# Attention with geometric and dot heads: V blocks two half-steps back everywhere, turns behind them, rows of maxima on GpSimd's queue

## The chip, the cores and the metric

The kernel runs on one core of one Trainium2 chip. The metric is the device time of one execution in microseconds (us), lower is better; times are given as the median of the runs shown.

## The reference

One layer on x of 2 x 2048 x 256, all f32. Attention has 16 heads of 16 channels, causal, and each head attends twice over the same tokens:

```python
std_logits = einsum('bhqd,bhkd->bhqk', q, k) * scale
geo_logits = einsum('bqhi,bkhi->bhqk', read_lines, J_write) * inc_scale
std_out = softmax(mask(std_logits)) @ v
geo_out = softmax(mask(geo_logits)) @ geo_v
combined = (1 - gate) * std_out + gate * geo_out
x = layernorm(x + combined @ out_w + out_b)
x = layernorm(x + (silu(x @ wg.T) * (x @ wu.T)) @ wd.T)
```

`read_lines` and `J_write` are six numbers per head and token, made by products of four-vectors and scaled to length one.

## The kernel before

Three parts follow one another: `project` makes the operands and writes them to DRAM, `attend` computes both attentions, `finish` does the output product, the norms and the gated layer. The change is all in `attend`.

`attend` runs over 16 items (`ITEMS`): a batch and a pair of heads. An item has four query tiles of 512 columns; a query tile goes through its key blocks of 128 in steps, and a step has one or two groups. A group is called a half-step here and counted h = 0 to 35 (`PVS`, `NPV`). Most half-steps hold one key block and 512 query columns. The last three of a query tile lie on the diagonal: 512 columns, 384, and one that holds two blocks, of 256 and 128. The tiles end at h = 2, 9, 20 and 35 (`LAST_OF`), and each last step has one group only.

In a half-step TensorE (PE, `step`) computes the GEO scores (line 1036) and, for an item that comes later, one or two tiles of dot-product maxima (line 1074), then the DOT scores (line 1042). Scores of both heads stand in one of two PSUM buffers `ex`. ScalarE (ACT, line 1217) makes the exponentials of each, two per half-step, into one of eight buffers `prob`. On the diagonal GpSimd zeroes what the mask forbids (line 1004). PE then multiplies by V into PSUM `pv` (`times_v`, line 1131: the V block). Ahead of a tile's first V block it waits until VectorE (DVE) has taken the tile before out of `pv` (`take`, line 1303). Score matmuls wait until the exponential of the buffer is done, exponentials until V has read their buffer:

```python
def earlier(j):
    prev, ps = (at, s - 1) if s else (before, NSTEP - 1)
    if prev is not None and j < len(STEPS[ps][1]):
        times_v(*prev, ps, j, head)
```

So the V block of group j of the step before follows the scores of group j. Where a step has one group, both V blocks of the step before stand behind its scores, then comes that of its own in the next step's first half-step, and the second half-step of that step has none.

The softmax needs a bound on each query's DOT score. Maxima of key blocks are made on PE and reduced by DVE (lines 1233, 1236) for the item after. At half-steps 30 (EARLY, query tiles 0 to 2) and 9 (LATE, tile 3) there is a turn: DVE makes columns of negated maxima (`negm`), PE transposes them (line 1108), DVE casts the result to `mrow` (line 1295). The rows of `mrow` are then sent by four DMAs into rows of the query operands `gq` and `dq` (line 894), where the score matmul adds them. PE waits for EARLY's rows (`m_in[EARLY]`) ahead of the GEO scores of half-step 0 and for LATE's at half-step 21. In a turn there is a branch that is not taken with these inputs; it would compute maxima of GEO scores too.

The tiles of maxima and the turns use three PSUM banks in a ring (`Ring`), and each new use waits for the last one of its bank: the bank of the EARLY turn comes again a few tiles later, that of the LATE turn is that of the very next tile.

SyncE (SP) issues DMAs in a fixed order (`item` in `block.sync`): per item the stores of the four taken tiles, 24 operand loads and V for the item after the next, and the rows. The LATE rows stand after the store of tile 0, the EARLY rows at the end of an item, behind the last six operand loads:

```python
store(it, 2)
load(range(18, 24))
...
if it + 1 < ITEMS:
    rows(it + 1, EARLY, sets[(it + 1) % NSET])
```

GpSimd makes 24 masks an item and after tile 2's masks, in items 0 to 3, work put aside: in item 0 it loads the output weights, waits for them and loads a weight; in items 1 to 3 it converts a weight and loads the next.

## Time and profile before

| | us |
|---|---|
| median of 3 runs | 1793.87 |
| lowest, highest | 1790.86, 1795.01 |
| the profiled execution, its own time | 1791.5 |
| its span, first to last instruction | 1789.8 |
| busy: PE | 1609.8 |
| busy: ACT | 1217.1 |
| busy: DVE | 1073.1 |
| busy: GpSimd (POOL) | 337.2 |

The profile is of one execution. PE is busy for 90% of it, which is a mean over parts of different kinds: `attend`'s items run from about 278 to 1474 us, `project` before, `finish` after. A busy PE is not a PE at its peak, since the ends of pipelined matmuls are modelled; starts are measured. In a row of the timeline the word in brackets is the idle time ahead of the first instruction and what ended it; "issue" means that the profile shows nothing that was waited for.

### The profile page before, as it was taken

What the parts mean: (1) busy time and instruction counts of PE and PEld (TensorE: products, weight loads), DVE (VectorE), ACT (ScalarE), POOL (GpSimd) and SP (SyncE); (2) the same over time, 40 slices, a digit from 0 to 9 for tenths busy, and PEclk for the clock granted to TensorE, in tenths of its full rate; (3) what the DMA queues carried; (4) which work ended last, traced back from release to release, by engine and by line L of the source; (5) the groups of instructions that cost most, each with busy time, mean ns of one, the idle gap of its engine ahead of it and who ended that gap; (6) DMA issues with size and microseconds to landing.
All of it is one profiled execution on the core that took longest, in us unless ns stands there. A gap on an engine that the chain in (4) does not pass through costs nothing. (4 is left out here: it accounts for less than half of the span.)

```text
span 1789.8 us, 31799 instructions
## 1 busy us (share of the span) xinstructions
PE 1609.8 (90%) x11809; PEld 567.9 (32%) x11809; DVE 1073.1 (60%) x2621; ACT 1217.1 (68%) x1457; POOL 337.2 (19%) x479
## 2 busy tenths in 40 slices
PE   7897467998989999999999999999999988999997
PEld 4554212222222222222222222222222225555564
DVE  4775575665666666666667666666666514554433
ACT  3554406988979889888898888988889872112111
POOL 4432321211111111111101111111110133121000
PEclk9999658999999999999999999999999998999999
DMA  5665521221212112121121211212214013222000
GB/s 169 213 207 171 180 88 43 87 80 50 86 44 70 51 62 72 46 66 65 50 82 50 67 58 56 71 46 65 72 40 129 21 54 115 96 84 70 23 12 24
DMA packets 95579, 140.31 MB, mean 78 GB/s; under 512 B 6352, under 2 KB 64528, under 8 KB 93360
## 3 DMA queue, kind: packets, MB, share of 16 engines
q1 hardware_dynamic: 94208, 135.08, 22.9%
q0 software_dynamic: 624, 2.75, 0.6%
q8 instruction: 97, 1.59, 0.4%
q14 instruction: 74, 0.61, 0.1%
q10 hardware_dynamic: 576, 0.28, 0.1%
HBM read 81.96 MB, written 55.61 MB: 77 GB/s over the span
## 5 line engine op out<-in xcount | busy, mean ns | idle before, releaser
L1217 ACT ACTIVATE prob<-ex 128x1024 f32<-128x1024 f32 (+1 forms) x1152 | 1048.5, 978 | 193.2 <-PE ex L1036 183.2
L1236 DVE TENSOR_REDUCE mp<-mx 128x1 f32<-128x512 f32 x768 | 492.2, 685 | 257.9 <-PE mx L1074 257.7
L1131 PE MATMUL pv<-prob,va 128*32 128x512 f32 (+3 forms) x5120 | 576.5, 541 | 0.4 <-POOL prob L1004 0.4
L1004 POOL TENSOR_SCALAR_AFFINE_SELECT prob<-prob 128x256 f32<-128x256 f32 (+1 forms) x384 | 186.1, 485 | 1025.3 <-ACT prob L1217 1020.5
L1042 PE MATMUL ex<-dq,dk 34*128 34x512 bf16 (+7 forms) x2560 | 336.8, 349 | 24.6 <-ACT prob L1217 17.6
L1233 DVE CUSTOM_DVE_ANT_0 dull<-mx,mask_qk 128x128 f32<-128x128 f32 (+3 forms) x512 | 222.0, 487 | 127.2 <-PE mx L1074 127.1
L1036 PE MATMUL ex<-gq,gk 38*128 38x512 bf16 (+3 forms) x1280 | 219.5, 356 | 45.2 <-issue 18.8
L1074 PE MATMUL mx<-dk,dq 64*128 64x512 bf16 (+3 forms) x1280 | 228.0, 357 | 15.8 <-issue 12.4
L1036 PEld LDWEIGHTS ex<-gq,gk 38*128 38x128 bf16 x1280 | 56.8, 93 | 452.2 <-ACT prob L1217 372.8
L1131 PEld LDWEIGHTS pv<-prob,va 128*32 128x32 f32 x5120 | 114.3, 108 | 240.2 <-issue 217.5
L1561 ACT ACTIVATE sg<-pg 128x512 f32<-128x512 f32 x48 | 28.7, 597 | 219.7 <-PE pg L1501 219.5
L1042 PEld LDWEIGHTS ex<-dq,dk 64*128 64x128 bf16 (+1 forms) x2560 | 93.1, 94 | 190.5 <-ACT prob L1217 160.7
L574 POOL TENSOR_TENSOR sp<-d,sp 128x512 bf16<-128x512 f32 (+1 forms) x48 | 69.2, 1456 | 139.3 <-ACT sp L669 139.3
L1501 PE MATMUL pg<-y_t,wg_f 128*128 128x512 f32 x192 | 90.3, 593 | 1.1 <-ACT y_t L1544 1.1
L1517 PE MATMUL po<-wd_f,ht 128*128 128x256 f32 x384 | 85.0, 381 | 6.4 <-DVE ht L1629 6.4
L1501 PE MATMUL pg<-y_t,wu_f 128*128 128x512 f32 x192 | 90.2, 592 | 0.0
L593 PE MATMUL pn<-wv,xc 128*128 128x512 f32 x128 | 64.4, 628 | 23.5 <-DVE vn L745 15.7
L1074 PEld LDWEIGHTS mx<-dk,dq 64*128 64x128 bf16 x1280 | 65.7, 96 | 49.0 <-DVE mp L1236 14.4
L1629 DVE SCALAR_TENSOR_TENSOR ht<-pg,sg 128x512 f32<-128x512 f32 x48 | 33.0, 690 | 79.0 <-ACT sg L1561 79.0
L1517 PEld LDWEIGHTS po<-wd_f,ht 128*128 128x128 f32 x384 | 72.3, 190 | 18.3 <-issue 5.1
L612 PE MATMUL pr<-xc,wqk 128*128 128x512 f32 x128 | 62.1, 641 | 14.9 <-ACT sp L663 14.9
L1303 DVE COPY on<-pv 128x512 f32<-128x512 f32 x64 | 44.2, 691 | 34.6 <-PE pv L1131 34.6
(109 smaller groups left out, 906.1 us busy)
## 6 DMA issues: line engine op xcount, KB each, us to landing
values<-vn SPq DMA_DIRECT2D x32, 512.0 KB, 5.2
va<-values SPq DMA_DIRECT2D x16, 1024.0 KB, 18.5
raw<-on SPq DMA_DIRECT2D x64, 256.0 KB
parts_dot<-sp SPq DMA_DIRECT2D x32, 384.0 KB, 5.0
dq<-parts_dot SPq DMA_DIRECT2D x96, 128.0 KB
dk<-parts_dot SPq DMA_DIRECT2D x96, 128.0 KB
parts_geo<-sp SPq DMA_DIRECT2D x16, 288.0 KB, 2.8
gq<-parts_geo SPq DMA_DIRECT2D x96, 48.0 KB
```

Of the source, the lines that this page charges most:

```text
L574: g.tensor_tensor(out=sp3[m][0:n, SLOTS[m][2], :], in0=d32[m][0:n, :], in1=sp3[m][0:n, SLOTS[m][1], :], op=ALU.subtract).then_inc(p3_done, 1)
L593: pe.matmul(bank[:, 0, :], xc[par][:, k, tok], wv[:, k, :], start=k == 0, stop=k == NK - 1)
L1004: g.affine_select(out=cut, in_=cut, compare_op=ALU.is_ge, fill=0.0, base=0, pattern=[[0, nb], [1, P]], channel_multiplier=-1).then_inc(mas ...
L1036: last = pe.matmul(ex[:, n % 2, a * CH + at:a * CH + at + w], k_set[rows, keys], q_set[rows, queries], start=True, stop=True)
L1042: last = pe.matmul(ex[:, n % 2, a * CH + at:a * CH + at + w], k_set[rows, part, keys], q_set[rows, part, queries], start=part == 0, stop=p ...
L1074: last[a] = pe.matmul(mx[:, RING.bank[i], at:at + w], q_set[rows, 0, qb * P:(qb + 1) * P], k_set[rows, 0, k0:k0 + w], start=True, stop=True)
L1131: last = pe.matmul(pv[blk * VW:(blk + 1) * VW, CH - w:CH], sets[which]["v"][:, kb, blk * VW:(blk + 1) * VW], prob[UNIT_AT[s, j, kind] % NP ...
L1217: act.activation(prob[n % NPROB][:, :].rearrange("p (b c) -> p b c", b=2)[:, :, 0:w], ex[:, n % 2, :].rearrange("p (b c) -> p b c", b=2)[: ...
L1233: return v.tensor_tensor_reduce(out=scrap, in0=source, in1=mask_qk[:, CH - w:CH], scale=1.0, scalar=3 * MASKED, op0=ALU.add, op1=ALU.max, ...
L1236: return v.tensor_reduce(out=to, in_=source, axis=AX.X, op=ALU.max)
L1501: last = pe.matmul(pg[m % 2][:, i, :], w[:, k, m * P:(m + 1) * P], y_t[:, k, :], start=k == 0, stop=k == NK - 1)
L1517: last = pe.matmul(po[tt % 2][:, 0:D], ht[:, m, tt * P:(tt + 1) * P], wdf[:, m, :], start=m == 0, stop=m == NM - 1)
```

## The change

Three things change. Every half-step now has exactly one V block, that of two half-steps before (`BEHIND`). A turn on PE stands behind the V block of its half-step instead of ahead of it; DVE's takes move so that each follows the new place of its tile's last V block. And the rows of maxima are issued by GpSimd instead of SP: LATE behind the masks of tile 1, EARLY behind those of tile 2 and ahead of the work put aside, the first item's EARLY ones ahead of its first mask.

```diff
+BEHIND = 2
...
 (SP)
-                rows(it, LATE, sets[it % NSET])
...
-                if it + 1 < ITEMS:
-                    rows(it + 1, EARLY, sets[(it + 1) % NSET])
...
-            rows(0, EARLY, sets[0])
...
 (GpSimd)
+            def rows(it, part, to):
+
+                g.wait_ge(mrow_ready[part], it + 1)
+                g.sem_inc(g_passed, 1)
+                n, first = PART_BLOCKS[part], PART_FIRST[part] * P
+                cols = slice(first, first + n * P)
+                for a in range(2):
+                    geo = to["geo"][0][HALF * a + GEO_ROWS:HALF * a + GEO_FULL, cols]
+                    dot = to["dot"][0][HALF * a + DOT_MINOR:HALF * a + DOT_MINOR + 2, 1, cols]
+                    for kind, dst in ((GEO, geo), (DOT, dot)):
+                        at = (2 * kind + a) * 2 * n
+                        g.dma_start(dst.rearrange("p (k t) -> p k t", t=P), mrow[part][at:at + 2 * n, :])\
+                         .then_inc(m_in[part], 16)
...
+                    if u == (LAST_OF[1], 0, DOT):
+                        rows(it, LATE, sets[it % NSET])
                     if u == (LAST_OF[NQT - 2], 0, DOT):
+                        if it + 1 < ITEMS:
+                            rows(it + 1, EARLY, sets[(it + 1) % NSET])
                         if has_aside:
                             aside(it)
...
+            rows(0, EARLY, sets[0])
...
 (PE)
-                def earlier(j):
-                    prev, ps = (at, s - 1) if s else (before, NSTEP - 1)
-                    if prev is not None and j < len(STEPS[ps][1]):
-                        times_v(*prev, ps, j, head)
+                def earlier(h):
+                    if h >= BEHIND:
+                        times_v(*at, *PVS[h - BEHIND], head)
+                    elif before is not None:
+                        times_v(*before, *PVS[h - BEHIND], head)
...
-                    if to and h in TURN:
-                        turn(it, to, TURN.index(h))
...
-                    earlier(j)
-                for j in range(groups, 2):
-                    earlier(j)
+                    earlier(h)
+                    if to and h in TURN:
+                        turn(it, to, TURN.index(h))
...
-            times_v(*static(LAST_ITEM), NSTEP - 1, 0, False)
+            for h in range(NPV - BEHIND, NPV):
+                times_v(*static(LAST_ITEM), *PVS[h], False)
...
 (DVE)
-                        if j == 0:
-                            if s == 0 and not head:
-                                take(it - 1, NQT - 1, False)
-                            for qt in range(NQT):
-                                if s - 1 == LAST_OF[qt]:
-                                    take(it, qt, head)
+                        if h == PV_AT[LAST_OF[NQT - 1], 0] + BEHIND - NPV and not head:
+                            take(it - 1, NQT - 1, False)
+                        for qt in range(NQT - 1):
+                            if h == PV_AT[LAST_OF[qt], 0] + BEHIND:
+                                take(it, qt, head)
```

PE at the end of query tile 2, from the last DOT scores of half-step 20 to the V block of half-step 22, before (`pv` rows are V blocks, `ex` rows scores, `mx` rows maxima; `m_in1` is the semaphore of the LATE rows):

```order
L1042 MATMUL ex<-dq,dk 128x128 x4
L1131 MATMUL pv<-prob,va 32x512 [waits masked]
L1131 MATMUL pv<-prob,va 32x512 x3
L1131 MATMUL pv<-prob,va 32x384 [waits masked]
L1131 MATMUL pv<-prob,va 32x384 x3
L1036 MATMUL ex<-gq,gk 128x512 [waits ex_done,m_in1]
L1036 MATMUL ex<-gq,gk 128x512
L1074 MATMUL mx<-dk,dq 128x512 [waits mx_free] x2
L1042 MATMUL ex<-dq,dk 128x512 [waits ex_done]
L1042 MATMUL ex<-dq,dk 128x512 x3
L1131 MATMUL pv<-prob,va 32x256 [waits masked]
L1131 MATMUL pv<-prob,va 32x256 x3
```

The same place in the change:

```order
L1131 MATMUL pv<-prob,va 32x512 [waits masked]
L1131 MATMUL pv<-prob,va 32x512 x3
L1036 MATMUL ex<-gq,gk 128x512 [waits ex_done,m_in1]
L1036 MATMUL ex<-gq,gk 128x512
L1074 MATMUL mx<-dk,dq 128x512 [waits mx_free] x2
L1042 MATMUL ex<-dq,dk 128x512 [waits ex_done]
L1042 MATMUL ex<-dq,dk 128x512 x3
L1131 MATMUL pv<-prob,va 32x384 [waits masked]
L1131 MATMUL pv<-prob,va 32x384 x3
L1036 MATMUL ex<-gq,gk 128x512 [waits ex_done]
```

The block of 384 columns has moved from half-step 20 to 21, and the next, of 256 and 128, from 21 to 22, where there was none.

PE at the LATE turn, half-step 9, from the end of the branch on; first before:

```order
L1098 UNCONDITIONAL_BRANCH
L1108 MATMUL mx<-ident,negm 128x128 [waits mx_free,negm_ready1]
L1131 MATMUL pv<-prob,va 32x512 [waits masked]
L1131 MATMUL pv<-prob,va 32x512 x3
L1131 MATMUL pv<-prob,va 32x384 [waits masked]
L1131 MATMUL pv<-prob,va 32x384 x3
L1036 MATMUL ex<-gq,gk 128x512 [waits ex_done]
L1036 MATMUL ex<-gq,gk 128x512
L1074 MATMUL mx<-dk,dq 128x128 [waits mrow_ready1,dot_in1]
```

and in the change:

```order
L1098 UNCONDITIONAL_BRANCH
L1108 MATMUL mx<-ident,negm 128x128 [waits mx_free,negm_ready1]
L1036 MATMUL ex<-gq,gk 128x512 [waits ex_done]
L1036 MATMUL ex<-gq,gk 128x512
L1074 MATMUL mx<-dk,dq 128x128 [waits mrow_ready1,dot_in1]
```

The V block of 512 columns now stands ahead of the branch and the one of 384 a half-step later, so that between the transpose and the maxima that wait for `mrow_ready1` only the GEO scores are left.

GpSimd in item 1, from the masks of tile 2 to those of tile 3, in the change (before, the same rows without the four of `mrow`):

```order
L999 AFFINE_SELECT prob<-prob 128x2x128 [waits ex_done] x4
L999 AFFINE_SELECT prob<-prob 128x4x128 [waits ex_done] x2
L975 DMA gq<-mrow 2x12x128 [waits mrow_ready0]
L975 DMA dq<-mrow 2x12x128
L975 DMA gq<-mrow 2x12x128
L975 DMA dq<-mrow 2x12x128
L961 CAST wg_f<-w_int 128x1536 [waits w_load]
L955 DMA w_int<-in_wu 128x2x768 [waits w_conv]
L999 AFFINE_SELECT prob<-prob 128x2x128 [waits ex_done] x4
```

The LATE rows stand likewise behind the masks of tile 1. GpSimd now waits for both turns between its masks, and the weight's conversion stands behind the EARLY rows.

## Rows read from the trace of the kernel before

**Rows 1.** Windows, one item from its first GEO score to the next item's (columns: stretch, engines' busy us, PE clock).

```profile
728.34:802.71 74.37, 70.00 (x642) 18.04 (x643) 48.92 (x126) 65.52 (x72) 11.63 (x24) 1.00 0.18 59
```

**Rows 2.** Timeline of PE, two full half-steps (start us, us, engine line op, tiles, shape, count).

```profile
792.91 0.39 PE L1036 MATMUL ex<-gq,gk 38*128 38x512 bf16 x2
793.90 1.06 PE L1131 MATMUL pv<-prob,va 128*32 128x512 f32 x8
794.90 0.39 PE L1036 MATMUL ex<-gq,gk 38*128 38x512 bf16 x2
```

**Rows 3.** Timeline, ACT's longest stretch without a pause.

```profile
791.37 7.39 ACT L1217 ACTIVATE prob<-ex 128x1024 f32<-128x1024 f32 x8 [0.45 <-PE ex L1036]
```

**Rows 4.** Timeline, end of item 6 and start of item 7, the take among it.

```profile
798.76 0.34 PE L1036 MATMUL ex<-gq,gk 38*128 38x256 bf16 x4
799.58 1.71 PE L1131 MATMUL pv<-prob,va 128*32 128x512 f32 x16
802.71 0.39 PE L1036 MATMUL ex<-gq,gk 38*128 38x512 bf16 x2 [1.42 <-issue]
803.69 0.86 PE L1131 MATMUL pv<-prob,va 128*32 128x256 f32 x16
804.61 0.69 DVE L1303 COPY on<-pv 128x512 f32<-128x512 f32 x1
814.42 0.39 PE L1036 MATMUL ex<-gq,gk 38*128 38x512 bf16 x2
```

**Rows 5.** Timeline, end of query tile 1 with the LATE turn in it.

```profile
820.24 0.34 PE L1036 MATMUL ex<-gq,gk 38*128 38x256 bf16 x4
821.35 0.33 PE L1108 MATMUL mx<-ident,negm 128*128 128x128 f32 x1 [0.43 <-DVE negm L1276]
821.72 0.28 DVE L1295 CAST mrow<-mx 32x128 bf16<-32x128 f32 x1 [0.42 <-PE mx L1108]
829.04 0.39 PE L1036 MATMUL ex<-gq,gk 38*128 38x512 bf16 x2
```

**Rows 6.** Timeline of PE, end of query tile 2, no turn in it.

```profile
842.78 0.34 PE L1036 MATMUL ex<-gq,gk 38*128 38x256 bf16 x4
851.05 0.39 PE L1036 MATMUL ex<-gq,gk 38*128 38x512 bf16 x2
```

**Rows 7.** Timeline, half-step 30 with the EARLY turn in it.

```profile
788.55 0.39 PE L1036 MATMUL ex<-gq,gk 38*128 38x512 bf16 x2
790.05 0.29 DVE L1295 CAST mrow<-mx 96x128 bf16<-96x128 f32 x1 [0.42 <-PE mx L1108]
790.66 0.66 SPq L894 DMA_DIRECT2D gq<-mrow  x1
790.94 0.39 PE L1036 MATMUL ex<-gq,gk 38*128 38x512 bf16 x2
```

**Rows 8.** Waits of PE's scores (columns: waiter, releaser, us in total, times, longest).

```profile
PE ex L1036 <- issue: 18.8, 12, 3.5
PE ex L1036 <- DMA dq<-mrow: 8.5, 1, 8.5
```

**Rows 9.** Timeline of PE, its last work ahead of the first item.

```profile
265.02 4.21 PE L1074 MATMUL mx<-dk,dq 64*128 64x512 bf16 x7 [0.52 <-DVE mp L1233]
```

**Rows 10.** Timeline of GpSimd, items 0 and 1.

```profile
323.33 0.59 POOL L987 DMA_DIRECT2D ob<-in_out_b  x1
330.93 0.71 POOL L974 DMA_DIRECT2D w_int<-in_wg  x1 [7.01 <-DMA ob<-in_out_b]
395.34 1.46 POOL L980 CAST wg_f<-w_int 128x1536 f32<-128x1536 int32 x1
```

**Rows 11.** DMA issues (KB of one, median us from issue to landing).

```profile
wo<-in_out_w POOLq DMA_DIRECT2D x1, 256.0 KB, 4.8
```

**Rows 12.** The instructions of tile mrow (ns: least, median, most).

```profile
L894 SPq DMA_DIRECT2D gq<-mrow x64: 607/662/3921, 261.0 to 1416.8; - x64
```

**Rows 13.** Windows, around the first score of item 2.

```profile
428.20:435.00 6.80, 5.75 (x40) 2.02 (x42) 3.53 (x6) 3.87 (x5) 1.26 (x4) 0.50 0.03 5
```

More of the change, by code:

```diff
@@ L881, in store @@
                             on[qt % 2][:, :]).then_inc(on_st[qt % 2], 16)
-            def rows(it, part, to):
-                q.wait_ge(mrow_ready[part], it + 1)
-                q.sem_inc(passed, 1)
-                n, first = PART_BLOCKS[part], PART_FIRST[part] * P
-                cols = slice(first, first + n * P)
-                for a in range(2):
-                    geo = to["geo"][0][HALF * a + GEO_ROWS:HALF * a + GEO_FULL, cols]
-                    dot = to["dot"][0][HALF * a + DOT_MINOR:HALF * a + DOT_MINOR + 2, 1, cols]
-                    for kind, dst in ((GEO, geo), (DOT, dot)):
-                        at = (2 * kind + a) * 2 * n
-                        q.dma_start(dst.rearrange("p (k t) -> p k t", t=P),
-                                    mrow[part][at:at + 2 * n, :])\
-                         .then_inc(m_in[part], 16)
             def item(it):
```

## The prediction

> **What bounds the kernel now.** I began with the windows, because sixteen like items make up two thirds of the program. One of them takes 74.4 us, with PE busy for 70.0, ACT for 65.5, DVE for 48.9 and GpSimd for 11.6, at a full PE clock [rows 1]. So PE and ACT together are the limit, and the question is where they stop each other. The timeline answers it. In an ordinary half-step PE needs 0.99 us from its GEO score to its V block (792.91 to 793.90) and 1.00 for that block, 1.99 in all [rows 2]. ACT at its quickest makes eight exponentials in 7.39 us, 1.85 for a half-step's two [rows 3]. PE therefore sets the pace there, by 0.14.
>
> Around the end of a query tile this is lost. At the end of item 6, PE scores half-step 35 in 0.82 us, then runs two V blocks in 1.71, and only then gives ACT something new [rows 4]. In the half-step after next it has scores but no V block, and ACT is the slower one. From GEO(35) to GEO(6) of the next item pass 15.66 us, 1.42 of them a stop ahead of GEO(0) that ends in "issue". That score waits for `m_in[EARLY]`. Ahead of the first item the same wait is named, 8.5 us for `dq<-mrow`; the twelve unnamed ones come to 18.8 us [rows 8]. I read those as the same wait, because the four row transfers are issued on SP behind the next operand loads. The cast that frees them ends at 790.34 (790.05 and 0.29), SP issues 0.3 later [rows 7], and GEO(0) starts at 802.71 [rows 4], 12.4 us after the cast.
>
> **Parts of the change.** PE's instruction count does not change; its V blocks are spread. I cost each half-step as scores plus V block, or as ACT's 1.85 where full-width scores stand and that is more. Scores with maxima: 0.99 full, 0.82 for 256+128 columns, and an estimated 0.9 for 384, between the two. V blocks: 1.00 full, 1.71 less 1.00 = 0.71 for 384 columns, 0.86 for 256+128 [rows 2, 4].
>
> *Item end, half-steps 35, 0, 1, 2, 3, 4, 5:* 1.82, 1.85, 1.76, 1.82, 1.85, 1.85, 1.99, together 12.94 against 15.66 less the stop of 1.42, that is 14.24. Gain 1.30.
>
> *End of tile 1, half-steps 9 to 12:* now 820.24 to 829.04, 8.80 [rows 5]. From GEO(9) to the turn's transpose pass 1.11, of which PE waits 0.43 for `negm`; the V block will stand ahead of the transpose and cover that. Half-step 9 becomes 0.68, 1.00 and the transpose's 0.33. A new wait takes part of it back: the maxima of half-step 10 use the turn's PSUM bank, so they wait for the cast, which ends 0.65 after the transpose starts. GEO(10) and the way to the maxima cover about 0.45, so I charge 0.2. Sum 2.01, 1.90, 1.85, 1.99 = 7.75. Gain 1.05.
>
> *End of tile 2, half-steps 20 to 23:* now 8.27 [rows 6], then 1.82, 1.85, 1.85, 1.99 = 7.51. Gain 0.76.
>
> *Half-step 30, the other turn:* 2.39 now [rows 7], about 2.3 then. Gain 0.1.
>
> *The takes.* The copy of `pv` used to have a half-step without V behind it; now the next V block follows. It lasts 0.69 and starts 0.06 after the block ends [rows 4], while the next block is due 0.92 later, or 0.75 in half-step 2. Four takes with DVE sometimes behind: 0.2 per item lost, from 0 to 0.8.
>
> That is 1.30 + 1.05 + 0.76 + 0.1 - 0.2 = 3.01 per item; 16 items, less one item end that has no successor, give 46.9 us.
>
> *Rows on GpSimd.* Nothing here shows a small transfer issued by GpSimd. The nearest rows: its issues last 0.59 and 0.71 [rows 10], and one of 256 KB landed 4.8 after issue, beside SP's loads [rows 11]. Four issues of 0.75 and 4.8 make 7.8 us after the cast. The transpose now starts 1.96 into half-step 30 and the cast ends 0.65 later, 0.3 to 0.4 into half-step 31; GEO(0) is due 9.7 after that half-step begins (three times 1.99, 1.9, 1.82), so 9.3 are there and the wait vanishes: 18.8. At 12.4 as now it would stay. A GpSimd DMA is by the Trainium skill ("SBUF — State Buffer", A bandwidth-pool intuition that's wrong) held up while VectorE has the shared port: 620 ns became 3100. The same page says that `tensor_reduce` takes no part in it, and the trace's DVE time here is mostly that; at 3.1 an issue my estimate would be 17.2 us after the cast and 7.9 lost at each item start.
>
> *Ahead of item 0* PE has finished its maxima at 269.23 (265.02 and 4.21) [rows 9] and idles 8.5 [rows 8]. Rows issued from 258 on land before that: 8.4.
>
> *Clock.* After the long stops ahead of items 2 and 3 the granted clock was 0.50, that is 1.2 GHz, for 6.8 us in the one shown [rows 13]. Without the stops: 2 us.
>
> *Masks.* GpSimd now stands at its wait for the EARLY maxima from half-step 20 to 30; no mask is due before 33, and V(33) in half-step 35. Four issues leave it free at about 3.4 into half-step 31. The weight conversions of items 1 to 3 come behind them, 1.46 and an issue of 0.7 [rows 10], free at 5.6; V(33) is due at 8.7, so they are covered. Not so in item 0: two issues (1.3), the wait of 7.0 for `out_b` [rows 10], another issue (0.7) and two masks at 0.48 (11.63 over 24 [rows 1]) end at 13.4. Loss 4.7, once.
>
> *SP and ACT:* SP loses eight issues an item and two waits; nobody waited for its other work, so nothing. ACT's order is the same; its probability buffers are freed by V(h-4), which ends before they are written.
>
> Sum: 46.9 + 18.8 + 8.4 + 2 - 4.7 = 71.4 us. The profiled execution took 1791.5, the median is 1793.9, 2.4 more; 1793.9 - 71.4 is 1722.5, and I say **1722 us**. What is late next is PE itself, at about 69 to 70 us of work in an item of 70.
>
> **Rivals.** *A, the evening out pays half.* PE and ACT alternate with two score buffers, and a half-step that ACT leads may be followed by one that PE leads with no reserve between. Against it: full half-steps already run at PE's 1.99 with such a coupling. 1722 + 23 = 1745.
>
> *B, the rows land as late as now,* 12.4 after the cast: another queue but the same engines. The Trainium skill ("DMA: Bandwidth & Descriptors", Issuing engines are not separate DMA queues) says that another issuing engine saves little but the issuing. For it speaks that the loads still run; against it the 4.8 of rows 11. In rows: 12.4 less 9.3 is 3.1, 15 times 47, and the 8 ahead of item 0: 1777.
>
> *C, slower: GpSimd's issuing is slow.* Then PE stops at each item start, and masks come late. With 4.8 for landing, the gain is gone where four issues take 9.3, 2.3 us each. The longest issue of such a transfer, on SP, took 3.9 [rows 12]; at that 20.4 less 9.3 is 11.1, 15 times 167: 1889. At 3.0 it is 1835. Against it stand 0.59 and 0.71, of GpSimd's own.
>
> *D, nothing changes,* because the double blocks were hidden: but ACT stands still there in the trace. *E, more:* takes, bank and item 0's masks cost nothing (11), and the half-steps that I give to ACT, some five an item, run at PE's pace, 0.1 less each (8): 1703.
>
> **How the numbers follow.** Forecast 0.63, A 0.16, B 0.10, C 0.06, D 0.02, E 0.03. The range, 1700 to 1754, holds forecast, A and E, a little over 0.8; its upper end adds 9 us to A for takes at their upper bound. Faster by over 0.2% (about what a measurement of this kernel can tell): forecast, A, B, E, 0.92. Slower: 0.06. Same: 0.02.
>
> **What would show it.** Right: an item at about 70 us; no "issue" stop of PE ahead of GEO(0); half-steps 9, 20, 35 at about 1.9; ACT's waits for PE's scores down by a third or more; the first score near 269; a stop of V for masks at the end of item 0 alone. Wrong: stops of PE on `mrow`'s rows, issues of over 2 us on GpSimd, V blocks waiting for the takes or masks in every item.

## The result, and the profile after

The changed kernel takes **1736.24 us** (median of 4 runs, 1734.81 to 1736.9), the kernel before 1794.24 beside it on the same chip (1790.86 to 1795.01). The ratio is 0.9679 with a 95% interval of 0.9662 to 0.9696: faster by 58 us. Forecast were 1722 us, 71.4 less; the range of 1700 to 1754 holds the result. The profiled execution took 1736.9 us and spans 1735.2, against 1789.8 for the span before, so the spans differ by 54.6.

The first view is the windows of one item, from its first GEO score to the next item's (columns as in [rows 1]). Of GpSimd's 17.56 us here, eight issues of rows are 4.6, and the weight's conversion put aside, which only items 1 to 3 have, is 1.5.

```profile
487.29:557.60 70.31, 69.75 (x648) 17.67 (x644) 49.15 (x127) 65.95 (x73) 17.56 (x34) 1.00 0.20 67
```

An item of 74.37 us has become one of 70.31, and PE does the same work in it: 69.75 us for 70.00. What PE lacks in the item is 0.56 us, where it was 4.37. The gain is idle time of PE and no less work.

The groups of instructions of the page show the same from ACT's side (columns: what it is and how often, busy us and mean ns of one, idle time ahead and what ended most of it):

```profile
L1217 ACT ACTIVATE prob<-ex 128x1024 f32<-128x1024 f32 (+1 forms) x1152 | 1055.7, 975 | 120.6 <-PE ex L1036 102.8
...
L1131 PE MATMUL pv<-prob,va 128*32 128x512 f32 (+3 forms) x5120 | 588.9, 541 | 3.9 <-POOL prob L999 2.5
...
L1036 PE MATMUL ex<-gq,gk 38*128 38x512 bf16 (+3 forms) x1280 | 219.7, 355 | 0.0
...
L975 POOL DMA_DIRECT2D gq<-mrow x64 | 36.8, 574 | 327.5 <-DVE mrow L1295 323.4
```

ACT's waits for GEO scores came to 183.2 us before, to 102.8 now. The GEO scores have no idle time ahead of them at all, where it was 45.2 us: the stops of 18.8 and 8.5 us [rows 8] are gone, and so are the waits for ACT ahead of these scores. One issue of rows on GpSimd takes 0.57 us.

Where did 54.6 us go, and where did 16.8 of the forecast's 71.4 stay? I read the two timelines at the same events: the first exponential, that of each item, the last V block, the take behind it and the first product of the gated layer in `finish` (tile `pg`; the output product stands ahead of it). The differences are taken before rounding.

| stretch | before | after | gained | forecast |
|---|---|---|---|---|
| up to the first exponential | 278.4 | 270.7 | 7.7 | 8.4 |
| items 0 to 14 | 1118.1 | 1064.9 | 53.2 | 61.3 |
| item 15, to the end of its last V block | 78.0 | 74.5 | 3.5 | 1.7 |
| last take to the first product of the gated layer | 14.3 | 20.6 | -6.4 | 0 |
| from there to the end | 301.0 | 304.3 | -3.4 | 0 |

The forecast's share of items 0 to 14 is 15 times 3.01, 18.8 for the stops, 2 for the clock, less 4.7 for masks. What the 53.2 are made of:

* The stops ahead of GEO(0), 18.8.
* The evening out. An ordinary item without a stop took 72.89 us and now takes 70.31, 2.58 less; 15 times that is 38.7.
* The clock, 3.4. Before, items 2 and 3 took 2.0 and 1.4 us more than the others even without their stops. Behind the stops ahead of them, of 3.54 and 2.53 us, the granted clock is 0.50, the lower level of 1.2 GHz, in [rows 13] and in the row below, from the start of item 3. In the change it is 1.00 at the start of both, and they take 70.3 us like the others.
* Less what item 0 lost, 4.1. It takes 76.15 us. Half-step 35 took 3.3 more than in other items, the masks. Its half-steps 0 to 3 took 2.6 more (before: 1.8); the granted clock is 0.50 up to about 279.
* Less what item 9 lost, 3.7. It takes 74.04 us. Before, it took 74.90, and 72.95 of that without the stop of 1.95 ahead of item 10: it had lost nothing.

```profile
506.70:510.10 3.40, 3.40 (x28) 1.16 (x26) 1.53 (x3) 2.05 (x2) 0.82 (x2) 0.50 0.00 0
```

The evening out, place by place. PE's row of GEO scores gives each half-step by its start (columns: start, us, instruction; the bracket is idle time and what ended it). Half-steps 0 to 5 of item 3:

```profile
485.46 0.34 PE L1036 MATMUL ex<-gq,gk 38*128 38x256 bf16 x4
...
487.29 0.39 PE L1036 MATMUL ex<-gq,gk 38*128 38x512 bf16 x2
...
489.04 0.34 PE L1036 MATMUL ex<-gq,gk 38*128 38x384 bf16 x2
...
490.93 0.34 PE L1036 MATMUL ex<-gq,gk 38*128 38x256 bf16 x4
...
491.90 1.06 PE L1131 MATMUL pv<-prob,va 128*32 128x512 f32 x8
492.90 0.39 PE L1036 MATMUL ex<-gq,gk 38*128 38x512 bf16 x2
...
493.35 0.59 PE L1042 MATMUL ex<-dq,dk 64*128 64x512 bf16 x4
...
494.66 0.39 PE L1036 MATMUL ex<-gq,gk 38*128 38x512 bf16 x2
...
495.32 0.11 PEld L1042 LDWEIGHTS ex<-dq,dk 64*128 64x128 bf16 x4 [0.56 <-ACT prob L1217]
495.33 0.61 PE L1042 MATMUL ex<-dq,dk 64*128 64x512 bf16 x4
...
496.66 0.39 PE L1036 MATMUL ex<-gq,gk 38*128 38x512 bf16 x2
```

The row at 485.46 is half-step 35 of the item before and GEO(6) follows at 498.70, so the stretch takes 13.24 us where 14.24 were [rows 4] and 12.94 were forecast. The half-steps 35, 0 and 1 are 1.83, 1.75 and 1.89; 2 to 5 are 1.97, 1.76, 2.00 and 2.04, where 1.82, 1.85, 1.85 and 1.99 were forecast. In half-step 2 the V block is the first of a tile and follows DVE's take, which in this item ran from 491.07 to 491.76; the scores alone would have let it start about 0.1 earlier. In half-step 4 the DOT scores start 0.67 behind the GEO scores, in half-step 3 0.45: their buffer's exponential is not done, since ACT is still behind from the half-steps that it led.

In the experiments the length of a half-step is taken from the start of its first exponential to that of the next one's, at the median over the items. It differs by up to 0.1 us from the distance of the GEO scores, and the sums are the same. Differences of a few us between two versions are near what repeated runs of one version differ by (`late_on_sp` ran from 1728.02 to 1737.2), so that the small ones are read from the items' lengths and not from the time.

### The profile page after: what moved, and what is told of

Its sections match the earlier page's. It is cut to its first block and busy times, and to the rows that moved or that the text cites. A ratio compares the mean times of both kernels' runs of the same rounds, so it can differ in the third digit from the quotient of the medians.

```text
span 1735.2 us, 31799 instructions
## 1 busy us (share of the span) xinstructions
PE 1610.5 (93%) x11809; PEld 564.2 (33%) x11809; DVE 1079.8 (62%) x2621; ACT 1224.3 (71%) x1457; POOL 407.9 (24%) x607
## 3 DMA queue, kind: packets, MB, share of 16 engines
q0 software_dynamic: 4720, 3.34, 0.9%
## 5 line engine op out<-in xcount | busy, mean ns | idle before, releaser
L1217 ACT ACTIVATE prob<-ex 128x1024 f32<-128x1024 f32 (+1 forms) x1152 | 1055.7, 975 | 120.6 <-PE ex L1036 102.8
L1131 PE MATMUL pv<-prob,va 128*32 128x512 f32 (+3 forms) x5120 | 588.9, 541 | 3.9 <-POOL prob L999 2.5
L1074 PE MATMUL mx<-dk,dq 64*128 64x512 bf16 (+3 forms) x1280 | 228.6, 357 | 20.1 <-issue 12.4
L1131 PEld LDWEIGHTS pv<-prob,va 128*32 128x32 f32 x5120 | 108.5, 108 | 235.2 <-issue 186.9
L975 POOL DMA_DIRECT2D gq<-mrow x64 | 36.8, 574 | 327.5 <-DVE mrow L1295 323.4
```

Source lines behind the costliest of these rows:

```text
L1074: last[a] = pe.matmul(mx[:, RING.bank[i], at:at + w], q_set[rows, 0, qb * P:(qb + 1) * P], k_set[rows, 0, k0:k0 + w], start=True, stop=True)
L1131: last = pe.matmul(pv[blk * VW:(blk + 1) * VW, CH - w:CH], sets[which]["v"][:, kb, blk * VW:(blk + 1) * VW], prob[UNIT_AT[s, j, kind] % NP ...
L1217: act.activation(prob[n % NPROB][:, :].rearrange("p (b c) -> p b c", b=2)[:, :, 0:w], ex[:, n % 2, :].rearrange("p (b c) -> p b c", b=2)[: ...
```

## The experiments

**1. Rows alone, 2. order alone.** The change has two halves, so each was run by itself. `rows_only` is the kernel before with the four DMAs of a turn issued by GpSimd, in the change's places (the diff is against the change; the takes and the last V blocks go back likewise):

```diff
-BEHIND = 2
...
-                def earlier(h):
+                def earlier(j):
+                    prev, ps = (at, s - 1) if s else (before, NSTEP - 1)
+                    if prev is not None and j < len(STEPS[ps][1]):
+                        times_v(*prev, ps, j, head)
...
+                    if to and h in TURN:
+                        turn(it, to, TURN.index(h))
...
-                    earlier(h)
-                    if to and h in TURN:
-                        turn(it, to, TURN.index(h))
+                    earlier(j)
+                for j in range(groups, 2):
+                    earlier(j)
```

> The kernel before with only the rows moved to GpSimd. My theory (the stops ahead of each item's first score are the rows waiting behind operand loads): the 18.8 us of stops and 8 us ahead of item 0 go, the drain gives 5.5 to 8 back and the masks at the end of item 0 about 5: near 1778, items of 73. Rival (evening out the V blocks makes nearly all of the gain, the rows land as late as they did): 1790 or more, stops of 1 to 3 us ahead of the first scores still there.

Measured 1774.98 us, 0.9903 of the kernel before (0.9887 to 0.992): 3 us below what was expected, and the rival, rows as late as before, fell. No GEO score waits ahead of an item, items without extra work take 72.89 us, and the first exponential is at 269.4:

```profile
564.59:637.48 72.89, 69.90 (x647) 17.98 (x644) 48.85 (x126) 65.52 (x72) 16.07 (x33) 1.00 0.18 61
```

`v_order_only` is the change with the rows back on SP in their old places:

```diff
                 store(it, 0)
+                rows(it, LATE, sets[it % NSET])
                 store(it, 1)
...
+                if it + 1 < ITEMS:
+                    rows(it + 1, EARLY, sets[(it + 1) % NSET])
...
 (GpSimd)
-                    if u == (LAST_OF[1], 0, DOT):
-                        rows(it, LATE, sets[it % NSET])
...
-                        if it + 1 < ITEMS:
-                            rows(it + 1, EARLY, sets[(it + 1) % NSET])
```

> The change with both sets of rows back on SP in their old places: only the order of V blocks, turns and takes is new. My theory: the half-steps around tile ends are as in the change (2.6 us an item saved), but the rows land 12.4 us after their cast and are due after 9.3, so that each item begins with a stop of about 3 us, and the 8 us ahead of item 0 stay: near 1782. Rival (the rows' landing follows the load of the queue and comes earlier with the shorter item): no stops, near 1745.

Measured 1830.09, ratio 1.0212 (1.0195 to 1.0229). The expectation missed by 48 us and on the wrong side of the kernel before. The waits of PE's scores (columns as in [rows 8]):

```profile
PE ex L1036 <- issue: 71.3, 13, 7.4
PE ex L1036 <- DMA dq<-mrow: 11.6, 2, 8.8
```

They were 18.8 and 8.5. The timeline at the end of item 6 shows how one arises, with rows of DVE, SP and PE in the order of time:

```profile
728.76 0.29 DVE L1295 CAST mrow<-mx 96x128 bf16<-96x128 f32 x1 [1.26 <-PE mx L1108]
...
729.87 1.87 SPq L291 DMA_DIRECT2D gk<-parts_geo  x3
731.86 0.66 SPq L895 DMA_DIRECT2D gq<-mrow  x1
...
736.47 0.34 PE L1036 MATMUL ex<-gq,gk 38*128 38x256 bf16 x4
...
737.29 1.07 PE L1131 MATMUL pv<-prob,va 128*32 128x512 f32 x8
743.88 0.61 PE L1036 MATMUL ex<-gq,gk 38*128 38x512 bf16 x2 [5.53 <-issue]
```

SP gets to the rows 2.8 us after the cast's end, because it is still issuing operand loads, and the score starts 14.8 us after the cast; in the kernel before those were 0.3 and 12.4 [rows 4, 7]. The score is also due earlier: about 9.3 us after the cast instead of 11. The stops are followed by half-steps at the lower clock. Half-steps 0 and 1 take 3.15 and 2.13 us at the median, 1.83 and 1.77 in the change, 1.7 an item. The 6.8 us from 743.88 were run at a mean granted clock of 0.77.

What follows: the halves are not additive. Rows alone give 1.0%, the order alone costs 2.1%, both together gain 3.2%. With the rows landing late the new order turns its own gain into a longer wait, since it brings GEO(0) forward and the cast back.

**3. Fewer DMAs on GpSimd's queue, `late_on_sp`.** New in the change's profile is the length of GpSimd's `DRAIN`, the instruction with which an engine ends a block, at the end of the attention part. The instructions of that line in the change (columns: count, ns least/median/most, start):

```profile
L814 POOLq DRAIN  x1: 8914/8914/8914, 1408.6 to 1408.6; - x1
...
L814 SPq DRAIN  x1: 467/467/467, 1411.6 to 1411.6; - x1
L814 SPq EVENT_SEMAPHORE  x1: 17/17/17, 1417.7 to 1417.7; - x1
```

and in the kernel before, where that line is 813:

```profile
L813 POOLq DRAIN  x1: 1162/1162/1162, 1472.9 to 1472.9; - x1
...
L813 SPq DRAIN  x1: 462/462/462, 1475.9 to 1475.9; - x1
L813 SPq EVENT_SEMAPHORE  x1: 17/17/17, 1476.5 to 1476.5; - x1
```

All engines leave the block together. Before, SP was last, and they left as it ended at 1476.4. Now SP ends at 1412.1 and all wait for GpSimd until 1417.5. That is 5.4 of the 6.4 us lost there. `late_on_sp` puts only the LATE rows back on SP, where they have time:

```diff
                 store(it, 0)
+                rows(it, LATE, sets[it % NSET])
...
-                    if u == (LAST_OF[1], 0, DOT):
-                        rows(it, LATE, sets[it % NSET])
```

> The change with the LATE rows back on SP; the EARLY rows stay on GpSimd. GpSimd's drain at the end of the attention part took 8.9 us with the change (133 DMAs issued by GpSimd in that part) and 1.2 before (5 DMAs). If the drain grows with the number of DMAs that GpSimd has issued, it is now near 5.1 us (69 DMAs), the following part begins 3.8 us earlier, and the time is near 1732. Rival: the drain is long as soon as GpSimd sends rows at all: then 8.9 us and 1736, no change. In both, an item stays at 70.3 us, since the LATE rows have more than 15 us before they are used.

Measured 1728.82 (1728.02 to 1737.2), ratio 0.9661 (0.9633 to 0.9688). `DRAIN` took 6.38 us: less than 8.9, so the rival fell, but more than the 5.1 of a length in proportion. The items took 70.29, so the LATE rows cost nothing on SP. Item 0 also lost less, 74.49 us.

**4. Both on SP, but early in its order, `rows_first_on_sp`.** If it is SP's order that makes rows late, they can stay on SP ahead of the last six loads, and the drain stays short (the calls on GpSimd go):

```diff
                 store(it, 2)
+                if it + 1 < ITEMS:
+                    rows(it + 1, EARLY, sets[(it + 1) % NSET])
                 load(range(18, 24))
...
             load_operands(q, parts, 1, sets[1])
+            rows(0, EARLY, sets[0])
             q.dma_start(sets[1]["v"][:, :, :], values[1]).then_inc(sets[1]["v_in"], 16)
```

> The change with both sets of rows on SP, but the EARLY ones issued ahead of the last six operand loads of an item, and ahead of the second item's V load at the start. My theory (what counted was to stand behind the loads, not which engine issues): no stops ahead of items, drain 1.2 us as before (5.5 less than the change, and 3 more in the part behind it), no late masks in item 0 (5 less), a little lost ahead of item 0: near 1722, faster than the change. Rival (a queue of its own is what made the rows land soon): stops of 1 to 3 us ahead of items, 1745 to 1765.

Measured 1733.0, ratio 0.9668 (0.9651 to 0.9684), 11 us over what was expected. The main point held: items of 70.30 us without a stop in steady state, rows landing 7.5 to 9.5 us after the cast in items 3 to 14, a `DRAIN` of 1.16. So most of the delay is the place behind the loads, and not SP. Missed was item 0, whose rows were issued from 259.28, 1.8 us after the cast's start, but behind all operand loads of set 1 in the queue, and came only for 275.24:

```profile
275.24 0.61 PE L1036 MATMUL ex<-gq,gk 38*128 38x512 bf16 x2 [6.58 <-DMA dq<-mrow]
```

and items 2 and 3, with stops of 1.60 and 0.26. Item 9 took 74.30 us.

**5. Masks ahead of the rows? `aside_first`.** GpSimd's row of item 0 in the change (timeline):

```profile
336.93 0.76 POOL L980 DMA_DIRECT2D wo<-in_out_w  x1
337.66 0.60 POOL L982 DMA_DIRECT2D ob<-in_out_b  x1
342.85 0.71 POOL L955 DMA_DIRECT2D w_int<-in_wg  x1 [4.59 <-DMA ob<-in_out_b]
343.56 2.65 POOL L999 TENSOR_SCALAR_AFFINE_SELECT prob<-prob 128x256 f32<-128x256 f32 x6
```

and PE beside it:

```profile
341.74 0.50 PE L1042 MATMUL ex<-dq,dk 64*128 64x256 bf16 x8
344.38 1.93 PE L1131 MATMUL pv<-prob,va 128*32 128x512 f32 x8 [2.14 <-POOL prob L999]
```

Six masks are late when GpSimd's wait for `ob` ends. The edit does the work put aside while GpSimd would wait for the maxima:

```diff
                     if u == (LAST_OF[NQT - 2], 0, DOT):
-                        if it + 1 < ITEMS:
-                            rows(it + 1, EARLY, sets[(it + 1) % NSET])
                         if has_aside:
                             aside(it)
+                        if it + 1 < ITEMS:
+                            rows(it + 1, EARLY, sets[(it + 1) % NSET])
```

> The change with GpSimd's work put aside ahead of the EARLY rows instead of behind them. My theory: item 0 loses 5 to 6 us at its end because the load of the output weights, which GpSimd waits for, now stands behind the wait for the turn of half-step 30 and delays the masks of tile 3; moved ahead of it, item 0 takes about 70.5 us and the time is near 1731. Rival (the loss in item 0 is its low clock and the V loads of the start): no change, 1736.

Measured 1733.63, ratio 0.9665 (0.9644 to 0.9685). Item 0 took 72.88 us instead of 76.15, the 3.3 of half-step 35 are gone. So the mechanism held, but not its size: 5 to 6 us had been expected, an item of 70.5 and a time of 1731. The 2.6 us in half-steps 0 to 3, at the lower clock, stayed, as the rival had it. The time is within the change's interval.

**6. The wait of the next maxima for the turn's bank, `banks_two`.** The forecast charged 0.2 us an item for it. Both turns get two places in the ring:

```diff
-                    at += 1 if part == EARLY else 3
+                    at += 2
```

> The change with both turns taking two places in the ring of PSUM banks (instead of one and three), so that the tile behind a turn is in another bank than the turn. My theory: half-step 10 (2.07 us) waits 0.3 for the cast, and that delay passes through DVE to the take of tile 1 and to the V block of half-step 12 (2.19); both go, 10 to 1.83 and 12 to about 2.04, 0.4 an item, 6 us in all: near 1730. Rival (DVE is simply full there): half-step 12 stays at 2.19 and the gain is 3 us or none.

Measured 1734.8 (1730.41 to 1739.94), ratio 0.9678 (0.9647 to 0.9709). The theory fell: half-step 10 went from 2.07 to 1.98, but 31 from 1.97 to 2.20, and the item from 70.31 to 70.41:

```profile
626.73:697.14 70.41, 70.00 (x647) 17.74 (x644) 49.12 (x127) 65.92 (x73) 16.06 (x33) 1.00 0.19 63
```

Half-step 31 is the one behind the EARLY turn, whose bank now comes again one tile sooner: one wait for a bank was exchanged for another.

**7. The turn ahead of the V block again, `turn_ahead`.**

```diff
+                    if to and h in TURN:
+                        turn(it, to, TURN.index(h))
                     if not nxt and (s, j) in PRODUCT_AT:
...
                     earlier(h)
-                    if to and h in TURN:
-                        turn(it, to, TURN.index(h))
```

> The change with the turn back ahead of the V block of its half-step; all else as in the change. My theory: PE waits 0.4 us for the negated maxima in half-step 9 again and half-step 30 is 2.39 again, while the wait of half-step 10 for the cast goes: in sum 0.2 to 0.3 an item lost, near 1740. Rival (the turn's place is worth the full 0.4 to 0.6 per item): 1744. Rival (worth nothing): 1736.

Measured 1741.64, ratio 0.9716 (0.9695 to 0.9738), near the 1740 expected; its interval just touches the change's, and the items decide:

```profile
630.22:700.88 70.66, 69.72 (x646) 17.54 (x642) 49.15 (x127) 65.88 (x73) 16.07 (x33) 1.00 0.19 63
```

Half-step 9 takes 2.41 for 1.92, 30 takes 2.38 for 2.23; 10 gets 0.25 back, and 11 and 12 together 0.05 (1.93 and 2.04 for 1.83 and 2.19). The turn's place is worth 0.35 us an item, some 5 us in all. These rows also give the price of the bank in the change, where half-step 10 waits for the cast: half-steps 10 to 12 take 6.09 us there and 5.79 here. At the end of tile 2, where there is no turn, the same three, 21 to 23, take 5.80 in the change. So the wait costs 0.3 an item and not the 0.2 charged, and most of the excess of half-step 12 is its; `banks_two` took only 0.09 of it away.

**8. A first combination, `best1`.** Item 9 had shown a new stop. Before, DVE's first reciprocal of the denominators ran from 947.13, at the end of item 8, and the work behind it fell into the stop of 2.19 us ahead of GEO(0) of item 9. In the change, on the timeline:

```profile
907.70 3.34 DVE L307 RECIPROCAL den<-den 128x512 f32<-128x512 f32 x1
...
911.08 0.69 DVE L309 TENSOR_TENSOR den<-den,den_gate 128x512 f32<-128x512 f32 x1
911.69 2.48 DVE L1236 TENSOR_REDUCE mp<-mx 128x1 f32<-128x512 f32 x4
...
912.43 0.39 PE L1074 MATMUL mx<-dk,dq 64*128 64x512 bf16 x1 [2.21 <-DVE mp L1236]
```

With nothing to cover it, the 4 us of DVE hold up the maxima's banks and PE with them. In `rows_only`, with the old order and no stops, PE waits 1.56 us at this place and item 9 is 1.8 us long. `best1` takes the rows of `rows_first_on_sp`, but item 0's on GpSimd, and the ring of `banks_two`, and cuts the reciprocal in four pieces of 128 columns at four steps, the multiplication behind them:

```diff
+                    if s in DEN_PIECES and isinstance(it, int) and it == PAIRS_OF_HEADS:
+                        cols = slice(DEN_PIECES.index(s) * P, (DEN_PIECES.index(s) + 1) * P)
...
+                        v.reciprocal(late["den"][:, cols], late["den"][:, cols]).then_inc(late["rd"], 1)
```

> Both sets of rows on SP with EARLY ahead of the last six loads, but item 0's EARLY rows on GpSimd with a semaphore of their own; both turns take two places in the ring; the reciprocal of the first batch's denominators (3.3 us on DVE at the end of item 8) in four pieces in four steps. My theory, from the run with rows first on SP (1733): 5 us less ahead of item 0, 6 from the banks, 3 from the pieces, since PE stood still for 2.2 us behind the one long reciprocal: near 1719. Rival (these waits cover each other): above 1727.

Measured 1729.42, ratio 0.9645 (0.9626 to 0.9664); missed by 10, above the 1727 of the rival. The first piece came before its data:

```profile
894.14 0.95 DVE L1341 RECIPROCAL den<-den 128x128 f32<-128x128 f32 x1 [3.56 <-DMA den_gate<-gates]
```

So item 8 took 75.06 us and item 9 70.41: the stall had moved by one item.

**9. The take between the two reductions, `take_between`.** In half-step 12 the first V block of tile 2 waits for the take of tile 1. DVE did four pieces of maxima first. Here the take comes after two:

```diff
             def max_tiles_of(it, h, between=None):
                 for a in range(2):
+                    if a and between:
+                        between()
...
+                                max_tiles_of(it, h, take_now if h == PV_AT[LAST_OF[1], 0] + BEHIND else None)
```

> The change with one thing moved on DVE: in half-step 11 the take of tile 1 stands between the two heads' maxima instead of behind both. After the run with two places each in the ring left half-step 12 at 2.19 us, my theory is that the take waits behind DVE's maxima there (they end 0.35 us after the last V block of tile 1) and holds up the next tile's first V block: then half-step 12 falls to about 2.0, an item to 70.1, and the time is 3 us less, near 1733. Rival (PE is late in half-step 12 because of half-step 10's wait for the cast): 2.19 stays.

Measured 1736.18 (1731.26 to 1737.44), ratio 0.968 (0.9656 to 0.9704). Half-step 12 went from 2.19 to 2.13, the item from 70.31 to 70.24; the time shows nothing. I had expected 1733. The rival was that half-step 12 is late because of half-step 10's wait, and `turn_ahead` bears it out, with 1.82 and 2.04 for the two. In half-step 12 PE waits mostly for ACT:

```profile
510.22 0.39 PE L1036 MATMUL ex<-gq,gk 38*128 38x512 bf16 x2
...
510.89 0.61 PE L1042 MATMUL ex<-dq,dk 64*128 64x512 bf16 x4
511.47 1.07 PE L1131 MATMUL pv<-prob,va 128*32 128x512 f32 x8
512.47 0.39 PE L1036 MATMUL ex<-gq,gk 38*128 38x512 bf16 x2
```

That is the change's timeline: DOT starts 0.67 behind GEO again, and the row of its weight load says why:

```profile
510.88 0.11 PEld L1042 LDWEIGHTS ex<-dq,dk 64*128 64x128 bf16 x4 [0.33 <-ACT prob L1217]
```

**10. Is it bytes, recency or the number? `late_on_gp`** leaves GpSimd the small LATE rows (2 KB each) and gives SP the EARLY ones (6 KB), early in its order:

```diff
 (SP)
+                if it + 1 < ITEMS:
+                    rows(it + 1, EARLY, sets[(it + 1) % NSET])
                 load(range(18, 24))
...
 (GpSimd)
-                        if it + 1 < ITEMS:
-                            rows(it + 1, EARLY, sets[(it + 1) % NSET])
```

> LATE rows on GpSimd, EARLY rows on SP ahead of the last six operand loads. GpSimd issues 69 DMAs in the attention part as in the run with LATE on SP, but the small ones (2 KB instead of 6) and the last of them in item 15. If the drain follows the number of DMAs it is 6.4 us again; if it follows their bytes or rows it is well under that; if it follows how recently GpSimd last issued one it is near the 8.9 of the change. Time: 1733 of the run with rows first on SP, plus the drain above 1.2, that is 1736 to 1740.

Measured 1734.58, ratio 0.9676 (0.9655 to 0.9696), 1.4 us below the stretch expected. In `late_on_sp` GpSimd issued 64 rows of 6 KB, here 64 of 2 KB, either time 69 DMAs with the five others, and the `DRAIN` is the same to the nanosecond:

```profile
L814 POOLq DRAIN  x1: 6384/6384/6384, 1413.5 to 1413.5; - x1
```

So it is neither the bytes nor how long before the end the last one was issued: that was at 1325.6 us in `late_on_sp`, 80 ahead of the `DRAIN`, and here at 1362.0, 51 ahead.

**11. The second combination, `best2`**: LATE rows and items 1 to 15's EARLY rows on SP, the latter ahead of the last six loads; item 0's on GpSimd with a semaphore of their own; the take between; the reciprocal's four pieces at later steps (`DEN_PIECES = (16, 17, 18, 19)`), its multiplication in item 9.

> Rows on SP with EARLY ahead of the last six loads, item 0's on GpSimd; ring as in the change; the take of tile 1 between the heads' maxima; the long reciprocal in four pieces, later than in the run before (where the first piece waited for its DMA, 4 us of stop in item 8), the multiply in item 9. My theory: items of 70.1, no stop in items 8 and 9, no drain above 1.2 us, no late masks in item 0: 1722 to 1725. Rival (the pieces still wait for the load, or the take's place does nothing): 1729 as before.

Measured **1725.5** us (1723.48 to 1726.74, 5 runs), ratio 0.9621 (0.9604 to 0.9638), which is below the change's interval and half a microsecond above the stretch expected. It is the fastest version here.

```profile
557.04:627.28 70.24, 69.69 (x646) 17.69 (x643) 49.17 (x127) 65.94 (x73) 11.57 (x25) 1.00 0.18 63
```

```profile
L815 POOLq DRAIN  x1: 1486/1486/1486, 1404.5 to 1404.5; - x1
```

Item 0 takes 72.39 us, item 9 70.80, the first exponential is at 270.7. Left are stops of 1.71, 0.48, 0.61 and 0.48 ahead of items 2, 3, 9 and 10.

**12. The number of DMAs again, `more_dmas`**: `late_on_gp` with 32 more small DMAs on GpSimd, which copy a constant into a tile that nobody reads, 101 in all.

```diff
+        scrap = sb("scrap", [8, 2, P])
+        aimless = sem("aimless")
...
+                        for i in range(2):
+                            if it:
+                                g.wait_ge(aimless, it * 32)
+                            g.dma_start(scrap[:, i, :], ident[0:8, :]).then_inc(aimless, 16)
```

> The kernel with LATE rows on GpSimd and EARLY ones on SP, and two more DMAs of 4 KB per item on GpSimd that copy a constant to a tile nobody reads: 101 DMAs by GpSimd in the attention part. The drain so far: 1.16 us with 5 DMAs, 1.49 with 9, 6.38 with 69 (0.082 us for each), 8.91 with 133 (0.040 for each of the last 64). If it grows by 0.082 up to a ceiling, it is 8.9 to 9.0 us now; if its slope falls at some count below 100, it is 7.6 to 8; if the added DMAs do not matter, 6.4. The time is that of the run with 69, 1734.6, and the excess of the drain: 1736 to 1738.

Measured 1737.74 (2 runs), ratio 0.9704 (0.9676 to 0.9732).

```profile
L814 POOLq DRAIN  x1: 8996/8996/8996, 1414.0 to 1414.0; - x1
```

The length of this `DRAIN` over the number of DMAs that GpSimd issued in the block, in all fourteen traces, and the time from the last V block to the next matmul of PE:

| DMAs | traces | `DRAIN`, us | V block to next matmul, us |
|---|---|---|---|
| 5 | 3 | 1.16 | 2.32 |
| 9 | 2 | 1.49 | 2.32 |
| 69 | 2 | 6.38 | 5.26 |
| 101 | 1 | 9.00 | 7.87 |
| 133 | 6 | five times 8.91 or 8.92, once 9.24 (`aside_first`) | 7.79 to 8.12 |

From 5 to 101 it is a line of 0.082 us a DMA, and PE pays for it from somewhere above 9 DMAs on. At 133 it is near 9 still; why it stops growing was not tried. The number of DMAs is not all that a `DRAIN` depends on: in the two other parts of the program, where GpSimd issues none, its `DRAIN` took 2.46 us and 3.4 to 4.2. And it does not add up over the parts, since that of `finish` is as long with 133 DMAs before it (3.39 in the change) as with 5 (3.40 in `rows_first_on_sp`).

## Why the prediction was right, and where it was off

Right in sign, inside the range, too low by 14 us. Its steps in turn:

*Rows on GpSimd, 18.8 us: right.* The step's price was a little too high and its conclusion safe. In item 3 the cast ends at 478.04 and the last issue starts at 480.47:

```profile
477.75 0.29 DVE L1295 CAST mrow<-mx 96x128 bf16<-96x128 f32 x1 [1.26 <-PE mx L1108]
...
478.74 0.60 POOL L975 DMA_DIRECT2D gq<-mrow  x1 [20.13 <-DVE mrow L1295]
...
480.47 0.58 POOL L975 DMA_DIRECT2D dq<-mrow  x1
```

The time from issue to landing of these four (the instructions of tile `mrow`, from 478.5 to 481 us) is at most

```profile
DMA to landing us min/median/max: 2.2/2.3/4.2
```

and by the landings in the trace the 4.2 us are the last one's. So all have landed 6.6 us after the cast, where 7.8 were forecast, of 9.3 that are there; the median over the items is 6.6 as well. Rival B, rows as late as before, did not come about on GpSimd. What late rows cost is shown by `v_order_only`, where they stay on SP. The rule under B, in the Trainium skill ("DMA: Bandwidth & Descriptors", Issuing engines are not separate DMA queues), is not borne out here for small transfers that somebody waits for: on SP behind the loads it took 12.4 and 14.8 us from the cast to the score, on SP ahead of the last six loads the rows landed after 7.5 to 9.5, on GpSimd after 6.6. The last issue starts 2.1 to 2.4 us after the cast in the last two, so the 2 us between them are not time of issuing. `rows_first_on_sp` shows that the place in SP's order gives most of the whole, and the change of issuer the rest.

*Rival C, slow issuing: did not happen.* 128 issues lasted between 544 and 747 ns. The slow case of the Trainium skill ("SBUF — State Buffer", A bandwidth-pool intuition that's wrong), 3100 ns beside a VectorE copy, is not seen here, with DVE busy for 49.15 of 70.31 us mostly in reductions. No run here has such copies beside issues throughout, so the rule itself is not judged.

*The evening out, 3.01 us an item forecast, 2.58 measured: the step that failed.* The text says: "I cost each half-step as scores plus V block, or as ACT's 1.85 where full-width scores stand and that is more." With the takes it charged 3.01. Place by place, item end, tile 1, tile 2 and half-step 30 gained 1.00, 0.85, 0.65 and 0.16 us (1.30, 1.05, 0.76 and 0.1 forecast). Taking the larger of the two in each half-step is too kind where they alternate. A half-step led by ACT leaves the next score matmul waiting for its buffer, as at 495.33 and 510.89, and PE's full block follows on top. That is rival A's mechanism, at 14% of the gain and not half of it. No run takes this coupling away by itself, so its share is read from the waits in the rows and is what is left beside the bank and the takes. The bank was charged with 0.2 and costs 0.3 by `turn_ahead`; the place of one take is worth 0.07 by `take_between`.

*Masks of item 0: the mechanism right, 4.7 forecast, 3.3 measured*, and `aside_first` shows that it is GpSimd's order alone. Too high was the wait for `ob`, 4.59 us in the change where the 7.0 of the trace before were taken over. *The first item: 8.4 forecast, 7.7 measured*; `rows_only` gives 9.0. *The clock: the mechanism right, 2 forecast, 3.4 measured* in items 2 and 3.

*Missing from the sum, all on the slower side:*

* The `DRAIN` of GpSimd, 5.4 us. "SP loses eight issues an item" was costed, GpSimd's 128 more issues were costed one by one, and what they leave behind at the block's end was not. Its length goes with the number of GpSimd's DMAs, as far as 101 of them. On the trace before it read 1.16 us and was hidden behind SP's.
* Item 9's reciprocal, 3.7 us (2.3 to 4.0 in the other kernels that have it whole and the new order). This stop had been covered by the very wait that the change takes away. It could have been found: the 3.34 us of DVE stand in the trace of before, just ahead of the stop of 2.19.
* 3.4 us in `finish`. Its length from the gated layer's first product to the end lies between 300.4 and 307.5 us from kernel to kernel, also where the `DRAIN` is short. In the profiled execution four DVE instructions there take 7.01 us beside GpSimd's work; all instructions of that line take 21.3 us, 16.0 before. But `best2` has 304.7 us with 15.7 in them. Whether that belongs to the change stays open.

The books: 6.4 behind the last take, 3.7 for item 9, 3.4 in `finish`, the evening out of items 0 to 14 (45.2 less 38.7, that is 6.5), 0.8 in item 0's first half-steps and 0.7 at the start make 21.5 us. The masks (1.4), the clock (1.4), item 15 (1.8) and small things (0.1) were better than forecast by 4.7. The difference, 16.8, is the one between 71.4 and 54.6. That the result lies as near as it does is in part luck: terms left out and terms too high stand on both sides.

## What to carry to other kernels

A change that removes waits brings work forward everywhere, so list what is due earlier and what lay under the removed wait: here the order alone lost 2.1% until its rows came sooner, and a 3.3 us reciprocal became visible. Small transfers that an engine waits for belong ahead of bulk loads in the issuing order, and if they go to GpSimd, count them: at 69 and more of them the end of the block came 3 to 6 us later. Where two engines of nearly equal pace alternate in the lead, charge more than the larger of the two per step: here 14% of the gain was missing, part of it by this.

## What the runs showed of the hardware

GpSimd's `DRAIN` at the end of the attention part grew by 0.082 us per DMA that it had issued there, from 1.16 us at 5 to 9.0 at 101, and was 8.9 to 9.2 at 133; at 69 it was the same whether 64 of them were of 2 or of 6 KB. Four transfers of 6 KB had landed 6.6 us after their data were ready when GpSimd issued them, 7.5 to 9.5 when SP did so ahead of six operand loads, and behind these loads the engine that waited for them went on 12.4 us after. DVE's reciprocal of 128x512 took 3.34 us, a copy of that shape 0.69. A stop of 5.53 us of PE was followed by a mean granted clock of 0.77 over 6.8 us, stops of 3.54 and 2.53 by 0.50 in the rows behind them; where the stops were taken away, the clock there was 1.00.
